# Two mixtures of experts: 23 tiles of 512 rows become 16 tiles of 512 rows and 7 of 256, large tiles first

## What is computed

```python
# block 0 (F = 352): top 2 of softmax(xt @ router_w)
h = gelu(xt @ w1[e]) * (xt @ v1[e]);  y = h @ w2[e]
out = sum over the two experts of weight * y + bias
# block 1 (F = 512): top 2 of softmax(xf @ Wr + br), weights normalised
h = gelu(xf @ Wi[e] + bi[e]) * sigmoid(xf @ Wg[e] + bg[e])
r = xf + h @ Wo[e] + bo[e]
y = (r - mean(r)) * rsqrt(var(r) + 1e-12) * gamma[e] + beta[e]
out = sum over the two experts of weight * y
```

## Time and profile before

| | before |
|---|---|
| median of 3 runs | 1089.29 us (1084.53 to 1096.25) |
| span of the profiled execution | 1101.2 us |
| PE busy | 980.5 us, 89% |
| DVE busy | 852.7 us, 77% |
| ACT busy | 620.6 us, 56% |
| POOL busy | 572.2 us, 52% |
| moved by DMA | 170.37 MB, mean 155 GB/s |
| mixture 1, first to last matmul | about 479 to 649 us |
| mixture 2, first to last matmul | about 835 to 1064 us |

### The profile page before, as it was taken

The page is one execution under the profiler, slowest core; times in us unless marked ns, Lnnn a source line. Parts: engine busy times, 40 slices in busy tenths (PEclk is TensorE's granted clock), DMA queues, the critical chain, the costliest instruction groups (busy, mean ns, idle before and its releaser), DMA issues. The chain is left out here.

```text
span 1101.2 us, 18065 instructions
## 1 busy us (share of the span) xinstructions
PE 980.5 (89%) x5608; PEld 634.8 (58%) x5608; DVE 852.7 (77%) x1910; ACT 620.6 (56%) x1248; POOL 572.2 (52%) x631
## 2 busy tenths in 40 slices
PE   5789999999999999989999964999996999999960
PEld 4542344343434344368888853756655888888850
DVE  7556899999979999435555548699992899999975
ACT  6115788888868888843333326333333666777642
POOL 7220687443435442015555556378782576777770
PEclk9995999999979999999999985699997999999985
DMA  6736566353535532216666635034312677687719
GB/s 209 300 104 193 160 193 209 101 169 113 170 101 170 178 116 88 87 58 195 207 197 187 205 95 146 20 108 126 93 44 82 180 214 208 208 224 220 218 56 236
DMA packets 121521, 170.37 MB, mean 155 GB/s; under 512 B 18801, under 2 KB 80594, under 8 KB 118354
## 3 DMA queue, kind: packets, MB, share of 16 engines
q1 hardware_dynamic: 94290, 110.94, 35.1%
q0 software_dynamic: 18688, 54.08, 14.3%
q10 hardware_dynamic: 8448, 4.20, 1.5%
HBM read 106.71 MB, written 63.76 MB: 155 GB/s over the span
## 5 line engine op out<-in xcount | busy, mean ns | idle before, releaser
L1667 DVE TENSOR_REDUCE nmax<-ps 128x1 f32<-128x512 f32 x512 | 324.8, 683 | 50.2 <-PE ps L1028 45.6
L1297 ACT ACTIVATE stage<-ps 128x512 f32<-128x512 f32 x512 | 274.4, 594 | 75.6 <-PE ps L1022 69.6
L841 POOL DMA_INDIRECT token_y<-stage,ids_now x184 | 182.7, 993 | 130.0 <-DVE stage L1723 58.3
L1028 PE MATMUL ps<-stage,stage 32*128 32x512 f32 x512 | 189.1, 521 | 14.1 <-DVE nmax L1667 12.8
L1022 PE MATMUL ps<-stage,stage 32*128 32x512 f32 x512 | 172.3, 496 | 9.0 <-ACT stage L1297 7.5
L797 POOL DMA_INDIRECT slots_x<-xn,pos x128 | 154.5, 1207 | 40.7 <-issue 39.6
L1168 PEld LDWEIGHTS ps<-stage,stage 128*128 128x128 f32 (+1 forms) x1288 | 164.9, 191 | 13.5 <-issue 1.8
L1168 PE MATMUL ps<-stage,stage 128*128 128x128 f32 (+1 forms) x1288 | 170.9, 275 | 1.5 <-issue 1.2
L1022 PEld LDWEIGHTS ps<-stage,stage 32*128 32x128 f32 x512 | 70.3, 188 | 158.0 <-ACT stage L1297 125.9
L324 PE MATMUL ps<-stage,stage 128*128 128x512 f32 x322 | 141.1, 438 | 3.6 <-issue 3.6
L1123 PE MATMUL ps<-stage,stage 128*32 128x512 f32 x1024 | 144.2, 637 | 0.0
(11 more groups left out here) (226 smaller groups left out, 1537.4 us busy)
## 6 DMA issues: line engine op xcount, KB each, us to landing
stage<-halves_w SPq DMA_DIRECT2D x23, 1024.0 KB
stage<-halves_w SPq DMA_DIRECT2D x23, 704.0 KB
stage<-slots_x SPq DMA_DIRECT2D x46, 260.0 KB
stage<-q_halves SPq DMA_DIRECT2D x32, 256.0 KB
halves_w<-stage POOLq DMA_DIRECT2D x16, 512.0 KB
k_halves<-stage SPq DMA_DIRECT2D x24, 256.0 KB
q_halves<-stage SPq DMA_DIRECT2D x24, 256.0 KB
stage<-k_halves SPq DMA_DIRECT2D x128, 48.0 KB
```

The source lines that it names most:

```text
L841: pool.indirect_dma_start(out=token_y, out_offset=bass.IndirectOffsetOnAxis(ap=ids_now[:, r, q:q + 1], axis=0), in_=ysb[:, r, q, :], in_of ...
L1028: pe.matmul(ps[:, (0, 1, 7)[bank_of(i)], :], head_rows(Qs, g2, j2)[:, t * P:(t + 1) * P], head_rows(Ks, g2, j2), start=True, stop=True).th ...
L1297: act.activation(probs[:, t % 2, j, :], ps[:, 2 + bank_of(i), :], ACT.Exp, scale=SCALE).then_inc(exp_set, 1)
L1667: dve.tensor_reduce(nmax[:, g % 2, at:at + 1], ps[:, (0, 1, 7)[bank_of(i)], :], AX, ALU.max, negate=True).then_inc(max_set, 1)
```

## The change

The unit of allocation becomes 256 rows. An expert with n rows gets as many large tiles (512, a pair of units) as fit and, where a half or less is left over, one small tile (256). 16 large and 7 small tiles always suffice, 39 units, so that 9984 slots take the place of 11776. All large tiles stand first, in the order of their experts, then the small ones; both mixtures run them in this order. There are 23 tiles as before. For a small tile the x load, the turn, the up products, the activations, h, the statistics and the residual work on 256 columns or 2 quarters where they worked on 512 or 4, and 2 scatters take the place of 4. The weights, the biases, gamma and beta are loaded for each tile as before. Waits on counts of rows follow from sums over tiles (`rows_until`, `stored_until`, `all_stored`). The zeroed space shrinks with the slots.

```diff
-TILES = 23
+UNIT = TILE // 2
+BIG, SMALL = 16, 7
+TILES = BIG + SMALL
+UNITS = 2 * BIG + SMALL
+SLOTS = UNITS * UNIT
+ORDER = list(range(TILES))
+ROWS = [4 if t < BIG else 2 for t in ORDER]
...
-                    sp.dma_start(xg[:, r, :, :].rearrange("p k d -> p (k d)"),
-                                 slots_x[L][bass.ds(i * TILE, TILE), :].rearrange("(p k) d -> p (k d)", p=P)
+                    a, K = first_row(i), ROWS[i]
+                    sp.dma_start(xg[:, r, 0:K, :].rearrange("p k d -> p (k d)"),
+                                 slots_x[L][a:a + K * P, :].rearrange("(p k) d -> p (k d)", p=P)
...
-                        c = slice(col + at, col + at + M)
-                        split3(pe, ps[0:M, bank + 2 * par, :], wu[:, r, 0, c], wu[:, r, 1, c],
-                               gT_hi[:, r, :], gT_lo[:, r, :]).then_inc(done[L], 1)
+                        c, W = slice(col + at, col + at + M), ROWS[i] * P
+                        split3(pe, ps[0:M, bank + 2 * par, 0:W], wu[:, r, 0, c], wu[:, r, 1, c],
+                               gT_hi[:, r, 0:W], gT_lo[:, r, 0:W]).then_inc(done[L], 1)
...
-                    for q in range(4):
+                    K = ROWS[i]
+                    for q in range(K):
                         mm = pe.matmul(ps[:, 5 + r, q * P:(q + 1) * P], hT[0:M, par, q * P:(q + 1) * P],
...
                 link(dve.tensor_tensor(posw[:, :, :], ps[:, 0, :].rearrange("p (c e) -> p c e", e=EXPERTS),
-                                       spread(off[:, :], 1, W3), ALU.add))
+                                       spread(pair_rows[:, :], 1, W3), ALU.subtract))
+                link(dve.scalar_tensor_tensor(posj[:, :, :], posw[:, :, :], 0.0, spread(jump[:, :], 1, W3),
+                                              ALU.is_ge, ALU.mult))
+                link(dve.tensor_tensor(posw[:, :, :], posw[:, :, :], spread(pair_end[:, :], 1, W3), ALU.add))
+                link(dve.tensor_tensor(posw[:, :, :], posw[:, :, :], posj[:, :, :], ALU.add))
...
-                for q in range(4):
+                for q in range(ROWS[TILES - 1]):
                     scatter(TILES - 1, 0, (q,))
```

More of the change, by code:

```diff
@@ L55, in build @@
     DX = D + 2
-    slots_x = [nc.dram_tensor(f"slots_x{L}", [TILES * TILE, DX], F32, kind="Internal").ap() for L in range(2)]
-    TOKENS, TOKEN_ROW = SEQS * SEQ, TILES * TILE
+    slots_x = [nc.dram_tensor(f"slots_x{L}", [SLOTS, DX], F32, kind="Internal").ap() for L in range(2)]
+    TOKENS, TOKEN_ROW = SEQS * SEQ, SLOTS
     token_y = nc.dram_tensor("token_y", [TOKEN_ROW + 2 * TOKENS, D], F32, kind="Internal").ap()
@@ L204, in build @@
         raw_halves = take_r(2, 2, F1)
-        take(NZ * DX - 18 * SEQ)
+        take(LOADS_AT + LOADS - 22 * SEQ)
         Hi = take_r(2, SEQ)
@@ L320, in rows_of, with first_row, rows_until, stored_until @@
             return tile[:, b * QT:(b + 1) * QT, :] if isinstance(b, int) else tile[:, bass.ds(b * QT, QT), :]
+        def first_row(i):
+            t = ORDER[i]
+            return t * TILE if t < BIG else (2 * BIG + t - BIG) * UNIT
+        def rows_until(i):
+            return sum(ROWS[:i])
+        def stored_until(i):
+            return 16 * sum(ROWS[i % 2:i:2])
+        def all_stored(r):
+            return 16 * sum(ROWS[r::2])
         def split3(pe, out_ap, w_hi_ap, w_lo_ap, x_hi_ap, x_lo_ap, start=True, stop=True):
@@ L636, in _ @@
             fill(causal[:, :], 1.0)
-            fill(before8[:, :, :], 1.0)
+            fill(before9[:, :, :], 1.0)
             fill(half[:, :], -0.5)
@@ L848, in rows @@
                         rows_of_tile(i, r)
-                        scatter(i, r)
+                        scatter(i, r, range(ROWS[i]))
                     rows(0, 0)
@@ L1139, in turn @@
                         pe.wait_ge(glo_set[L], i)
-                    for q in range(4):
+                    for q in range(ROWS[i]):
                         mm = pe.transpose(ps[:, 0, q * P:(q + 1) * P], xg[:, r, q, 0:D], ident[:, :])
@@ L1166, in down @@
                             pe.wait_ge(y_read[L], i - 1)
-                    for q in range(4):
+                    K = ROWS[i]
+                    for q in range(K):
                         mm = pe.matmul(ps[:, 5 + r, q * P:(q + 1) * P], hT[0:M, par, q * P:(q + 1) * P],
-                                       wdn[0:M, r, f, :], start=(f == 0 and q == 0), stop=(f == last and q == 3),
+                                       wdn[0:M, r, f, :], start=(f == 0 and q == 0), stop=(f == last and q == K - 1),
                                        skip_group_check=True)
@@ L1378, in experts @@
                 if L == 1:
-                    weighted(TILES - 1, 0, range(4))
+                    weighted(TILES - 1, 0, range(ROWS[TILES - 1]))
             def chunk(m, s, k, now):
@@ L1720, in weighted @@
                     if not (isinstance(i, int) and i < 2):
-                        dve.wait_ge(y_stored[L][r], (i - r) * 32)
-                    for q in range(4):
+                        dve.wait_ge(y_stored[L][r], stored_until(i))
+                    for q in range(ROWS[i]):
                         ins = dve.scalar_tensor_tensor(ysb[:, r, q, :], ps[:, 5 + r, q * P:(q + 1) * P],
@@ L1761, in center @@
                     dve.wait_ge(vec_in[r], (k + 1) * 32)
-                    dve.wait_ge(est_chain, i * 10 + 10)
-                    for q in range(4):
+                    dve.wait_ge(est_chain, rows_until(i + 1) + 6 * (i + 1))
+                    for q in range(ROWS[i]):
                         ins = dve.scalar_tensor_tensor(y[:, q, :], y[:, q, :], emean[:, q:q + 1], vecs[:, r, 0, :],
```

204 lines of the change are left out of this document (120 added, 84 removed).

## The result

The changed kernel takes 1046.9 us (median, 1042.42 to 1050.66) beside 1086.9 us before (1084.09 to 1096.25); the ratio is 0.962, 95% interval 0.957 to 0.967. It is 40 us faster, where 47.5 were forecast and the forecast time was 1042.

The account below looks back on a forecast made before the run. PE's columns were taken to bound both mixtures. Terms −21 −22 −3.5 −4.4 +3.4 sum to −47.5, taken from the runs' median 1089.3, not the profiled 1101.2, giving 1042 us; range 1030 to 1063.

Parts of the forecast that it names:

- PE's floor of a small tile: PE alone: 256-column matmuls 0.13 us, a chunk 1.21, a small tile 3.9 in mixture 1 and 5.1 in mixture 2.
- rival E: Both mixtures: a half-wide matmul costs 0.19 us, a chunk 1.58; 1054 us, chance 0.03.
- Mixture 1, the up loads: Up-weight buffers in mixture 1: 5.3 us load plus 3.4 use, 8.7 per two small tiles; −21 us.
- Mixture 2, the loop: Mixture 2: normalising, gamma and beta, bias columns, gelu: 13.4 us per two small tiles; −22 us.
- It fits, with little air: DMA rings in both mixtures: small tiles need 262 and 269 GB/s, scaled windows give 300 and 283, best window 331.
- Narrower ACT, DVE and POOL operations lie under PE and the loads: Small tiles: these engines' work stays covered; DVE, next in line, needs 4.4 us plus some 1, below 6.7.
- rival D: Both mixtures: waits make PE run small tiles at 1.2 GHz; 1092 us, slower, chance 0.04.
- B: Both mixtures: loads hide and PE's floor rules, though mixture 2 takes 6.0 a tile; 1035 us, chance 0.13.
- C: Both mixtures: loads come half as late again, 8.0 and 10.8 us; 1060 us, chance 0.22.
- G: Both mixtures: loads alone fill the old period, only −4.5 us is left; 1084.8 us, chance 0.05.
- A: Both mixtures: buffer loops set small tiles, 4.35 and 6.7 us each; 1042 us, own range 1034 to 1051, chance 0.53.
- Ends and routing: Fewer scatters behind the mixtures, −3.5 and −4.4 us; longer DVE chain in the second routing, +3.4.

Follow-up runs that it names:

- e3: Changed kernel without loading gate and up weights of tiles 18 to 22 in both mixtures; one run, 1035.6 us.
- e5: Changed kernel with mixture 1 alone reordered: two large, five times large, large, small, then four large, two small; 1047.3 us, ratio 0.962.
- e9: Changed kernel with the edits of e6 and e3 together: three buffers in mixture 2, no up loads for tiles 18 to 22; one run, 1037.7 us.
- e1: Changed kernel with gamma and beta, and their wait for normalising, issued later in SP's queue in mixture 2, behind x; 1045.0 us, ratio 0.959.
- e6: Changed kernel with a third buffer for mixture 2's down weights and bias columns, gamma and beta as in e1; 1047.9 us, ratio 0.963.
- e2: Changed kernel with both mixtures reordered: two large tiles, then large, large, small seven times; 1061.8 us, ratio 0.975.
- e7: Changed kernel with the seven small tiles ahead of the sixteen large ones in both mixtures; one run, 1055.0 us.

## Why the prediction was right, point by point

- **The bound before and the parts.** Right: the time came out of the two mixtures and the ends behind them, and each term has its sign. The forecast gain was 7.5 us too good (40 of 47.5). The time, 1046.9, lies inside the range and inside the likeliest case's own (1034 to 1051). That it is only 5 off is in part luck: the median before came down by 2.4 with a fourth run.
- **PE's floor of a small tile.** 0.12 apart and 1.15 a chunk where 0.13 and 1.21 were put: the line through 384 and 512 columns was good, and rival E (0.19) is out.
- **Mixture 1, the up loads (−21, measured −18.6).** The mechanism was right: three waits, in every second tile. They came in tiles 18, 20 and 22, and not in 17, 19 and 21 as laid out; and the layout starts 18, 20 and 22 some 0.5 ahead of what its own 3.9 a tile allows PE. The term was mis-sized in two of its parts, the load (5.3 put; 5.7, 6.2, 5.3 measured) and the stretch from up's first matmul to the next issue (3.4 put; 3.7 and 4.1 measured). Three turns of the loop at some 0.9 are the 2.7. That the loads are the whole of it is shown by e3 (−5.5 without them) and e5 (147.4 without succession). The estimate of 3.7 us for 704 KB by the Trainium skill (SBUF — State Buffer, "The DMA setup-cost knee") was further off here than the 4.2 from the rows: a tile would not have waited by it.
- **Mixture 2, the loop (−22, measured −17.1).** This is the step that was most off. From tile 16's first gelu (957.88) to PE's end (1011.90) it is 54.0, not 46.4, so that the term itself, 68.8 before, gave 14.8. Another 2.4 came from the large tiles, where nothing was put: from the first turn to tile 16's gelu it is 160.4 before, 158.0 after and 158.3 to 159.6 in the other kernels with the same order. That was luck; its cause stays open. The loop of the bias columns exists. Its two halves were put at 6.2 and 7.2; ahead of the long wait they measured 6.9 to 7.4 and 6.8 to 8.2. What failed is "It fits, with little air", by which only that loop was laid out. The rings carried the 264 GB/s (269 were needed), but a load of 1 MB took 8.2 us in them, for which the prediction has no term, and its loop is as long as the other. Without the up loads the stretch is 47.4 (e3), at clock 1.00, beside the 46.4 that was put. The prediction also left out that x and the output bias are issued behind the bias columns in the same queue, so that PE's turn waits too (8.3 us, 2.9 in e3). DVE's work per tile, put at 4.4 and some 1, is 5.6 (e9): that sum was good. That "Narrower ACT, DVE and POOL operations lie under PE and the loads" was not: with no load late, a tile takes 6.3 where the floor on PE was put at 5.1, and PE waits for h.
- **What the loop is made of.** The prediction took it as a wait for normalising. e1 and e6 show that it is no single wait: with that one gone SP waits for the down product and PE for the up weights (7.4 us), with that one gone too PE's waits are for h and the up weights, and with the up loads gone for h alone. Each step gave 0 to 5 us.
- **The clock (rival D).** It came in small: one fall in after, 0.60 over 990 to 997, with PE's longest wait (3.42 us), worth 2.7 us at most (an estimate: half of the 5.3 us from 992.9 on). Waits of 1.3 to 2.3 us in the same stretch left the clock at 1.00, but waits of that length did not always: in e2 and e7 falls came with or just behind 2.1 to 2.5 us, and in e2 a wait of 2.92 passed without one. So "a wait four times as long as any that I expect" was no safe distance. The Trainium skill (TensorE: Matmul & The Clock Gate, "Loop structure matters more than you think") shows a loop with a long wait for a DMA ahead of every matmul as one that runs cold. The waits here are shorter, and the small tiles as a whole did not run cold: PEclk is 1.00 in mixture 1 and 0.94 over those of mixture 2.
- **Rivals B, C and G.** B is what e3 shows for mixture 1 (146.0), and G fell with the gain itself. Mixture 1's small tiles, 33.7 us from tile 16's first up product (580.08) to the end, lie a third of the way from A (31) to C (39); mixture 2's, at 54.0, two thirds of the way from A (46.4) to C (57.2).
- **Ends and routing.** −3.1 and −4.6 for −3.5 and −4.4, +3.1 for +3.4. e7 shows that the ends follow the tiles that stand last: with large ones there they are as before. The routing's stage is 122.9 to 123.0 in nine of the ten experiments and 122.3 in the one with small tiles first, which fits that `pos` ends the stage's chain, as put: from the copy of `off` to the start of `pos` it is 3.61 us before and 6.83 after, 3.2 more, and the stage is 3.1 longer.
- **Against the median.** Taking the sum from the median and not from the profiled time was right: before's longer execution lost its time ahead of mixture 1, with attention at a lower clock in two stretches.

What stays open is why a load of 1 MB takes 8.2 us in mixture 2 and how much of the 6.6 us that e3 gives back is the clock's: no run changed the size of that load or its place in the queue alone.

## What to carry to other kernels

When an engine that was always busy gets less to do per tile, look for the loops through the buffers that its work used to cover, all of them, and lay them out tile by tile with two numbers each: from issue to use, and from use to the next issue. Then follow the order of the other engines at the new size: with no load late a small tile still took 6.3 us, with 5.6 us of work on DVE and a floor of 5.1 on PE. And where a loop spans two tiles, the order of short and long ones has to be tried: in mixture 1 in turn was better, 147.0 against 151.5 us in succession; in mixture 2 seven small tiles gave 17 us in succession and 1 us in turn.

## What the runs showed of the hardware that was not expected

- Down weights and bias columns (256 KB and 4 KB, waited for together) were used 4.0 to 4.7 us after the issue of the second in after, 4.9 to 7.1 in e1, where they stand closer behind a load of 1 MB, and 3.4 to 4.4 in e3, with no such load ahead of them but for the first.
- A load of 1 MB was used 8.1 and 8.2 us after its issue at a DMA share of 0.91 (264 GB/s), in the two rows shown.
- PE waits of up to 2.3 us between its matmuls left the granted clock at 1.00 over the small tiles of after, while in e2 and e7 falls to 1.2 GHz came with or just behind waits of 2.1 to 2.5, and a wait of 2.92 in e2 came without one. After the wait of 3.42 us half-wide matmuls stood 0.21 apart and not 0.12.
